# A stack of four graph layers on one core: the third layer's neighbour sum moved ahead of its weights, its bias carried in a column, and every engine's steps in a new sequence

## The chip, the core and the metric

The kernel runs on one core of a Trainium2 chip. A core has five engines that each work through an instruction list of their own: TensorE (PE) for matrix products and transposes, VectorE (DVE), ScalarE (ACT), GpSimd (POOL) and SyncE (SP), which issues most transfers. They meet at semaphores only. The metric is device time in microseconds for the whole launch, the median of several runs.

## What is computed

128 graphs of 128 nodes with 128 features each go through four layers. Each layer adds its result to its input and normalises every node's row to mean 0 and variance 1.

```python
x = _layernorm(x + _L0_gnn_ref(x, adj, ...))   # 25 nodes, 5 groups, two convolutions
x = _layernorm(x + _L1_gnn_ref(x, adj, ...))   # attention, 8 heads, log(adj + 1e-6) added to the scores
x = _layernorm(x + _L2_gnn_ref(x, adj, W, b))  # the layer that is changed here
x = _layernorm(x + _L3_gnn_ref(x, adj, ...))   # 5 rounds of a gated recurrent cell

def _L2_gnn_ref(node_features, adj_matrix, W, b):
    degree = jnp.sum(adj_matrix, axis=-1)
    d_inv_sqrt = jnp.power(degree, -0.5)
    d_inv_sqrt = jnp.where(jnp.isinf(d_inv_sqrt), 0.0, d_inv_sqrt)
    norm_adj = adj_matrix * d_inv_sqrt[:, :, None] * d_inv_sqrt[:, None, :]
    transformed = jnp.einsum('bnf,of->bno', node_features, W) + b
    return jax.nn.relu(jnp.einsum('bnm,bmo->bno', norm_adj, transformed))
```

## The kernel before

Four graphs make a **block**, and two blocks (a = half 0, b = half 1) make an **iteration**; there are 16 iterations and so 32 blocks. A tile of a block is 128 x 512. The loop runs 19 **passes**. In one pass three threads of work run beside each other, on different iterations: thread A is the attention of the iteration before (steps `x1_t`, `qkv`, `s`, `max`, `t`, `p`, `a`, `u`, `n`, `on`, `wo`), thread B is the first layer of the newest iteration and the third layer of the one or two before (`l0_...`, `adj_t`, `x2`, `x2_t`, `l2_t`, `l2_agg`), and thread R is the five rounds of the gated cell (`agg`, `r`, `r2`, `hn`, `in`, `z`, `z2`, `turn`, `begin`, `end`) for two blocks that are two to three rounds apart. The order of each engine's list is written out by hand: `MERGE` holds for each engine two strings of A, B and R, one for each half of a pass, which say from which thread the next step comes. The same two strings serve all 19 passes; in the first and last passes the steps of iterations that don't exist are left out, and a few steps of the last blocks are held back (`HELD`).

The third layer of a block runs so. `x2` (DVE): the second layer's normalised rows. `x2_t`: PE turns them with 4 transposes into the PSUM bank M2 (L958, a helper line for all transposes), ACT copies the result to `x2T` (L620). `l2_t`: PE multiplies by the weights (L1152), DVE adds the bias row out of M2 (`t_b`, L832), POOL multiplies each row by its `dinv` (`t_d`, L526). `l2_agg`: PE sums over the neighbours with `adjT` (L1157), ACT applies the second `dinv` and the relu (L677), DVE adds `x2` (`y3`) and takes the moments for the norm. The bank M2 is shared by all steps of thread B, so they follow each other in it. L996 is the gated cell's products, L1107 the scores, L610 the exponentials, L1124 the weighted sums of the attention, L1140 its output product, L1090 to L1094 the keys, queries and values, L1193 the cell's neighbour sum, L535 and L539 POOL's two operations per round of the cell (`h_lo`, `hd`), L714 a norm on DVE.

Of the kernel before, what the change touches and what calls it, by code (L numbers as in the profile page):

```python
# [7 lines left out]
ALU = mybir.AluOpType  # L8
# [17 lines left out]
LAYERS = 5  # L26
# [13 lines left out]
    deg=NG, deg_safe=2 * NG, deg_pow=NG, dinv=NG, x2t_mm=NG, x2_t=NG, t_mm=NG, t_b=NG, t_d=NG, a_mm=NG, a_relu=NG, y3=NG,  # L40
# [34 lines left out]
def first_third_steps(half):  # L75
    end, last, pair = (1 - half, 1 - half), (2 - half, 1 - half), (0, 0)
    second = [(*last, "x2_t", 0), (*last, "l2_t", 0), (*last, "l2_agg", 0), (*end, "adj_t", 0), (*end, "l0_add", 0)]
# [34 lines left out]
def body_steps(merge):  # L112

    out = []
    for half in range(NG):
        threads = dict(A=iter(attention_steps(half)), B=iter(first_third_steps(half)), R=iter(gated_steps(half)))
        out += [(thread, *next(threads[thread])) for thread in merge[half]]
        assert all(next(left, None) is None for left in threads.values())
    return out
# [9 lines left out]
def gnn_stack_kernel(nc, x, adj, nodemask, W1, b1, W2, b2, fusion_w, Wq, Wk, Wv, Wo, bo, L2W, L2b,  # L129
# [3 lines left out]
    with ExitStack() as ctx:  # L133
# [1153 lines left out]
```

## Time and profile before

| | us |
|---|---|
| three runs | 1687.17, 1689.47, 1689.93 |
| median | 1689.47 |
| span of the profiled execution, first to last instruction | 1687.2 |
| first product for keys in the first block | 34.1 |
| one pass (two blocks) in the steady stage | 99.9 |
| busy: PE, its weight loads, DVE, ACT, POOL | 1619.3, 1343.7, 1400.9, 1314.6, 790.3 |

The first 34 us load and turn the weights; from there to about 200 us the three threads start one after the other; from 200 to about 1500 us each pass has all three and repeats to 0.1 us; after that the threads run out and the last block's cell is alone. The page's busy time counts a PE instruction from its start to its modelled end, so the ends of neighbours overlap; the distance from one start to the next is the time that PE gives to it.

### The profile page before, as it was taken

How to read it: one execution, taken by the hardware profiler on the slowest of the kernel's cores; microseconds unless marked ns; L12 is line 12 of the kernel's file. 1: busy time of each engine (PE TensorE's matmuls, PEld its weight loads, DVE VectorE, ACT ScalarE, POOL GpSimd, SP SyncE). 2: the span in 40 equal slices, each digit the busy share in tenths (PEclk: the TensorE clock that was granted, in tenths of full speed). 3: DMA queues.
4: the chain of work that ended last, by engine and by line, in shares of the span. 5: the costliest groups of instructions: out<-in, count | busy, mean ns of one | idle time of the engine just before them, and what ended most of it. 6: DMA issues, size and time to landing. Idle time of an engine off the chain costs nothing.

```text
span 1687.2 us, 34433 instructions
## 1 busy us (share of the span) xinstructions
PE 1619.3 (96%) x12294; PEld 1343.7 (80%) x12294; DVE 1400.9 (83%) x3563; ACT 1314.6 (78%) x3147; POOL 790.3 (47%) x842
## 2 busy tenths in 40 slices
PE   8789999999999999999999999999999999999997
PEld 7568787887878788787887878888787888877776
DVE  5687888979789897989879798897978889797766
ACT  2568878887878888878887887878787888878766
POOL 3143544536454463544546354453645445354442
PEclk9899999999999999999999999999999999999999
DMA  3010100001010100101001010000101001000000
GB/s 95 20 42 1 30 26 17 27 14 42 14 30 14 28 28 14 30 26 30 14 20 36 14 31 26 18 26 14 43 13 30 25 17 27 14 26 14 13 1 20
DMA packets 84803, 40.97 MB, mean 24 GB/s; under 512 B 10629, under 2 KB 84634, under 8 KB 84634
## 3 DMA queue, kind: packets, MB, share of 16 engines
q1 hardware_dynamic: 84058, 38.62, 8.4%
q8 instruction: 99, 1.62, 0.4%
q14 instruction: 70, 0.57, 0.1%
q10 hardware_dynamic: 576, 0.15, 0.0%
HBM read 30.36 MB, written 8.39 MB: 23 GB/s over the span
## 4 chain that ended last, share of the span: by engine, by line
PE 82%; DVE 8%; ACT 7%; issue 1%; POOL 1%; SPq 0%; DMA 0%; POOLq 0%; DVEq 0%; ACTq 0%
PE RA L996 18%; PE RB L996 17%; PE Q L958 8%; PE RT L1193 8%; PE RT L958 4%; PE Q L1107 4%; PE Q L1124 3%; PE M L958 3%; PE Q L1140 2%; ACT x L553 2%; PE Q L1094 2%; PE Q L1090 2%; PE M L1157 2%; PE M L1152 2%; PE Q L1091 2%; PE M L1035 1%
## 5 line engine op out<-in xcount | busy, mean ns | idle before, releaser
L535 POOL TENSOR_TENSOR h_lo<-hT,h_hi 128x512 fp32r<-128x512 f32 (+1 forms) x163 | 205.9, 1264 | 561.0 <-ACT h_hi L636 488.3
L610 ACT ACTIVATE e_s<-Q,s_ng 128x128 f32<-128x128 f32 x1024 | 292.2, 398 | 42.2 <-DVE s_ng L803 42.1
L539 POOL TENSOR_TENSOR hd<-hT,nn 128x512 f32<-128x512 f32 x156 | 201.0, 1288 | 38.7 <-ACT nn L654 38.7
L811 DVE TENSOR_TENSOR p_s<-Q,adjTe 128x512 f32<-128x512 f32 x256 | 171.2, 684 | 15.5 <-PE Q L958 14.3
L803 DVE TENSOR_REDUCE s_ng<-Q 128x4 f32<-128x512 f32 x256 | 169.1, 682 | 14.0 <-PE Q L1107 12.3
L646 ACT ACTIVATE tr<-RA,b_rz 128x512 f32<-128x512 f32 (+1 forms) x160 | 113.7, 710 | 83.6 <-PE RA L996 83.6
L861 DVE SCALAR_TENSOR_TENSOR un<-tr,un 128x512 f32<-128x512 f32 (+1 forms) x164 | 115.1, 704 | 72.2 <-ACT un L650 71.7
L958 PE MATMUL Q<-ident,e_s 128*128 128x128 f32 x1024 | 154.0, 275 | 10.9 <-ACT e_s L610 10.8
L654 ACT ACTIVATE nn<-tr,wT 128x512 f32<-128x512 f32 (+1 forms) x164 | 118.0, 722 | 57.6 <-DVE tr L866 57.5
L958 PEld LDWEIGHTS Q<-ident,e_s 128*128 128x128 f32 x1024 | 122.3, 141 | 33.1 <-ACT e_s L610 16.6
L488 POOL TENSOR_TENSOR rs<-ve,half_neg 128x4 f32<-128x4 f32 x128 | 140.3, 1096 | 10.7
L996 PE MATMUL RA<-agg_hi,comp_hi 128*128 128x512 f32 (+1 forms) x320 | 140.9, 440 | 2.6 <-DVE agg_lo L856 0.9
L996 PE MATMUL RB<-h_hi,whh_hi 128*128 128x512 f32 (+1 forms) x320 | 143.1, 447 | 0.0
L1193 PE MATMUL RT<-a_bin,h_tok 128*128 128x128 f32 x1008 | 137.1, 279 | 0.6 <-ACT h_tok L634 0.2
L658 ACT ACTIVATE tz<-RB,b_rz 128x512 f32<-128x512 f32 (+1 forms) x160 | 111.8, 699 | 31.0 <-PE RB L996 28.9
L484 POOL TENSOR_SCALAR ve<-mv 128x4 f32<-128x4 f32 x128 | 41.1, 321 | 200.9 <-DVE mv L699 195.5
L1193 PEld LDWEIGHTS RT<-a_bin,h_tok 128*128 128x128 f32 x1008 | 124.7, 191 | 11.8 <-issue 4.6
L856 DVE TENSOR_TENSOR agg_lo<-RT,agg_hi 128x512 fp32r<-128x512 f32 (+1 forms) x159 | 108.3, 681 | 28.4 <-ACT agg_hi L642 24.9
L553 ACT ACTIVATE x<-y,nm,rs 128x128 f32<-128x128 f32 x254 | 104.3, 481 | 32.9 <-DVE nm L710 32.1
L875 DVE SCALAR_TENSOR_TENSOR hd<-tz,hd 128x512 f32<-128x512 f32 (+1 forms) x164 | 120.5, 736 | 7.3 <-ACT tz L658 3.3
L996 PE MATMUL RB<-h_hi,whh_lo 128*128 128x512 f32 (+1 forms) x320 | 125.7, 393 | 0.0
L996 PE MATMUL RA<-agg_lo,comp_hi 128*128 128x512 f32 (+1 forms) x320 | 125.1, 391 | 0.0
(237 smaller groups left out, 4429.2 us busy)
## 6 DMA issues: line engine op xcount, KB each, us to landing
adjn<-in_adj_dram SPq DMA_DIRECT2D x32, 256.0 KB, 2.9
xin<-in_x_dram SPq DMA_DIRECT2D x32, 256.0 KB, 3.4
adjr<-in_adj_dram SPq DMA_DIRECT2D x32, 256.0 KB, 3.1
out_dram<-x SPq DMA_DIRECT2D x32, 256.0 KB, 2.4
adjc<-in_adj_dram SPq DMA_DIRECT2D x124, 4.0 KB, 2.1
xs<-in_x_dram SPq DMA_DIRECT2D x120, 16.0 KB, 1.8
W1s<-in_L_gnn_W_dram SPq DMA_DIRECT2D x1, 640.0 KB, 4.9
W2s<-in_L_gnn_W_dram SPq DMA_DIRECT2D x2, 320.0 KB, 5.0
```

Source lines behind the costliest of these rows:

```text
L488: return pool.tensor_tensor(r[:, :], v[:, :], half_neg[:, 0, 0:GB], ALU.pow)
L535: pool.tensor_tensor(h_lo[g][:, c], hT[g][:, c], h_hi[g][:, c], ALU.subtract).then_inc(SG["h_lo"][g], 1)
L539: pool.tensor_tensor(hd[g][:, c], hT[g][:, c], nn[g][:, c], ALU.subtract).then_inc(SG["hd"][g], 1)
L553: ins = act.activation(o[:, b, :], y[:, b, :], ACT.Identity, bias=n[:, b:b + 1], scale=r[:, b:b + 1])
L610: ins = act.activation(e_s[:, j, c, :], Q[j][:, c * P:(c + 1) * P], ACT.Exp, bias=s_ng[:, j, c:c + 1])
L654: act.activation(nn[g][:, c], tr[g][:, c], ACT.Tanh, bias=bih[:, 2:3]).then_inc(SG["n_act"][g], 1)
L803: dve.tensor_reduce(s_ng[:, j, :], Q[j][:, :].rearrange("p (c k) -> p c k", c=4), AX_X, ALU.max, negate=True)\
L811: dve.tensor_tensor(p_s[:, j, :, :].rearrange("p (b h) q -> p b h q", b=2), Q[j][:, :].rearrange("p (b h q) -> p b h q", b=2, h=2), adjTe[ ...
L875: dve.scalar_tensor_tensor(hd[g][:, c], tz[g][:, c], 1.0, hd[g][:, c], ALU.add, ALU.mult).then_inc(SG["he"][g], 1)
L958: return pe.transpose(o, i, ident[0:rows, 0:rows])
L996: ins = pe.matmul(o[:, cs], weights, moving[:, cs], start=start and i == 0, stop=last is not None and i == len(pairs) - 1)
L1193: ins = pe.matmul(T[:, q * P:(q + 1) * P], src[:, q, :], a_bin[g][:, q, :], start=True, stop=True)
```

## The change

The third layer now sums over the neighbours first. POOL multiplies `x2` by `dinv` into columns 0 to 126 of a new tile `x2d` (step `l2_agg` on POOL, L607), and DVE writes `dinv` itself into column 127 (a second small instruction in step `x2`). PE takes `x2d` as it lies, with the nodes on the partitions, as the stationary side and `adjT` as the moving side (`l2_agg`, L1233), and the sum comes out turned; ACT copies it to `agg2T`; PE multiplies by the weights (`l2_t`, L1238); ACT applies `dinv` and relu as before. The 4 transposes per block, the bias addition on DVE and `t_d` are gone. A normalised row sums to zero, so its last feature is minus the sum of the others: the weights are prepared once with their last input row subtracted from the others (`l2_ext`, one DVE instruction), and the place of the last input row takes the bias, which the `dinv` column then carries through the sum. The pieces below are, in this order, POOL's, ACT's, DVE's (in `x2`, in `l2_t`, and once at the start) and PE's.

```diff
+                elif kind == "l2_agg":
+                    wait(pool, "dinv", it, 2 * g + 2)
+                    wait(pool, "x2", it, g + 1)
+                    pool.tensor_tensor(x2d[:, :, 0:P - 1], x2[g][:, :, 0:P - 1], dinv[g][:, :].unsqueeze(2).broadcast_to([P, GB, P - 1]), ALU.mult)\
+                        .then_inc(S["x2_d"], 1)
                 elif kind == "l2_t":
-                    wait(pool, "t_b", it, g + 1)
-                    wait(pool, "dinv", it, g + 1)
-                    pool.tensor_tensor(t_d[:, :, :], t_b[:, :, :], per_graph(dinv[g][:, :]), ALU.mult).then_inc(S["t_d"], 1)
-                elif kind == "l2_agg":
...
-                elif kind == "x2_t":
-                    wait(act, "x2t_mm", it, g + 1)
-                    act.activation(cols(x2T[g]), M2[:, :], ACT.Copy).then_inc(S["x2_t"], 1)
+                elif kind == "l2_agg":
+                    wait(act, "agg2_mm", it, g + 1)
+                    act.activation(cols(agg2T), M2[:, :], ACT.Copy).then_inc(S["agg2_t"], 1)
...
+                    wait_before(dve, "agg2_mm", it, g)
+                    dve.scalar_tensor_tensor(x2d[:, :, P - 1], deg[g][:, :], 0.0, deg_p[g][:, :], ALU.not_equal, ALU.mult)\
+                        .then_inc(S["dinv"], 1)
...
                 elif kind == "l2_t":
-                    wait(dve, "t_mm", it, g + 1)
-                    dve.tensor_tensor(t_b[:, :, :], M2[:, :].rearrange("p (b d) -> p b d", b=GB),
-                                      l2b_row[:, :].unsqueeze(1).broadcast_to([P, GB, P]), ALU.add).then_inc(S["t_b"], 1)
-                elif kind == "l2_agg":
                     wait(dve, "x2", it, g + 1)
                     wait(dve, "a_relu", it, g + 1)
...
+            dve.wait_ge(w_first, 16 * SQUARE_DMAS)
+            dve.tensor_scalar(l2_ext[:, 0:P - 1], stage[:, WL2, 0:P - 1], stage[:, WL2, P - 1:P], None, ALU.subtract).then_inc(w_ext, 1)
...
-                elif kind == "x2_t":
-                    wait(pe, "x2", it, g + 1)
+                elif kind == "l2_agg":
+                    wait(pe, "dinv", it, 2 * g + 2)
+                    wait(pe, "x2_d", it, g + 1)
...
-                        ins = turn(M2[:, q * P:(q + 1) * P], x2[g][:, q, :])
-                    ins.then_inc(S["x2t_mm"], 1)
+                        ins = pe.matmul(M2[:, q * P:(q + 1) * P], x2d[:, q, :], adjT[g][:, q, :], start=True, stop=True)
+                    ins.then_inc(S["agg2_mm"], 1)
```

At the start the bias transfer moves from the last of SP's weight transfers to the sixth (128 rows of one element in place of a row broadcast to all partitions), and PE turns the third layer's weights, out of `l2_ext`, with its second group of weights and no longer with its first.

The sequence is the second half of the change. `MERGE` has three strings per engine in place of two: one for passes 0 to 4 taken together, one that serves each of passes 5 to 12, one for passes 13 to 18 taken together. Its letters stand for finer lanes (on PE the cell's steps split into gates, `in`, `z` and the rest; on DVE and ACT the two blocks in the cell, and the attention's `max` and `p`, have lanes of their own), so steps can pass each other that had a fixed order.

```diff
+HEAD, TAIL = 5, 13
...
+    head, body, tail = MERGE[engine]
+    blocks = [(range(HEAD), head)] + [(range(n, n + 1), body) for n in range(HEAD, TAIL)] + [(range(TAIL, iters + LAG), tail)]
```

Three places where it shows. First PE in pass 1, between the first and the second block's attention. Before (L1140 is the first block's output product, `Q<-ident,x` the turning of the second block's rows, L1042 and L1046 the first layer's second weights for the next iteration, L1090 to L1107 keys, queries, values and scores of the second block):

```order
L958 MATMUL Q<-ident,o_ns 128x128 x4
L1140 MATMUL Q<-wT,on_ts 128x128 x4
L958 MATMUL Q<-ident,x 128x128 x4
L1042 MATMUL M<-hid_t,W2s 128x200 x2
L1042 MATMUL M<-hid_t,W2s 128x8x9 x2
L1046 MATMUL M<-hid_t,W2s 128x8x7 x2
L1046 MATMUL M<-hid_t,W2s 128x8x6 x4
L1090 MATMUL Q<-xT,wT 128x512
L1091 MATMUL Q<-xT,wT 128x512
L1094 MATMUL Q<-wT,xT 128x128 x4
L1107 MATMUL Q<-km,qT 128x256 x8
```

Now (the lines have moved by 85: L1225 is L1140, L1175 is L1090, L1192 is L1107, L1127 and L1131 are L1042 and L1046, L1120 is the first layer's first weights):

```order
L1225 MATMUL Q<-wT,on_ts 128x128 x4
L1041 MATMUL Q<-ident,x 128x128 x4
L1120 MATMUL M<-y_t,W1s 128x8x9
L1120 MATMUL M<-y_t,W1s 128x8x7
L1120 MATMUL M<-y_t,W1s 128x8x6 x2
L1175 MATMUL Q<-xT,wT 128x512
L1176 MATMUL Q<-xT,wT 128x512
L1179 MATMUL Q<-wT,xT 128x128 x4
L1192 MATMUL Q<-km,qT 128x256 x8
L1127 MATMUL M<-hid_t,W2s 128x200 x2
L1127 MATMUL M<-hid_t,W2s 128x8x9 x2
L1131 MATMUL M<-hid_t,W2s 128x8x7 x2
```

The first layer's second weights have moved from ahead of the second block's keys to behind its scores. Next PE at the end of a steady pass, around the attention's normalisation of block b (`Q<-ident,o_ts` and `Q<-ident,o_ns` are the transposes ahead of and behind it). Before:

```order
L1124 MATMUL Q<-p_s,vp 32x128 x16
L958 MATMUL Q<-ident,o_ts 128x128 x8
L996 MATMUL RB<-h_hi,whh_hi 128x512
L996 MATMUL RB<-h_lo,whh_hi 128x512
L996 MATMUL RB<-h_hi,whh_lo 128x512
L996 MATMUL RB<-agg_hi,comp_hi 128x512
L996 MATMUL RB<-agg_hi,comp_lo 128x512
L996 MATMUL RB<-agg_lo,comp_hi 128x512
L958 MATMUL Q<-ident,o_ns 128x128 x4
L958 MATMUL RT<-ident,x_0 128x128 x4
L1140 MATMUL Q<-wT,on_ts 128x128 x4
```

Now:

```order
L1081 MATMUL RB<-h_hi,whh_hi 128x512
L1081 MATMUL RB<-h_lo,whh_hi 128x512
L1081 MATMUL RB<-h_hi,whh_lo 128x512
L1209 MATMUL Q<-p_s,vp 32x128 x16
L1081 MATMUL RB<-agg_hi,comp_hi 128x512
L1081 MATMUL RB<-agg_hi,comp_lo 128x512
L1081 MATMUL RB<-agg_lo,comp_hi 128x512
L1041 MATMUL Q<-ident,o_ts 128x128 x8
L1041 MATMUL Q<-ident,o_ns 128x128 x4
L1041 MATMUL RT<-ident,x_0 128x128 x4
L1225 MATMUL Q<-wT,on_ts 128x128 x4
```

One of the six gate products' groups now stands ahead of the weighted sums, the other between them and the transposes, and none behind. Last POOL at the start of a steady pass, with the third layer of block b. Before:

```order
L493 TENSOR_SCALAR deg_z<-deg 128x10
L495 TENSOR_TENSOR deg_s<-deg,deg_z 128x10
L497 TENSOR_TENSOR pow<-deg_s,half_neg 128x10
L512 TENSOR_SCALAR adjTe<-adjT 128x512
L516 TENSOR_TENSOR x1b<-x,bo_row 128x512
L535 TENSOR_TENSOR h_lo<-hT,h_hi 128x512
L526 TENSOR_TENSOR t_d<-t_b,dinv 128x512
L539 TENSOR_TENSOR hd<-hT,nn 128x512
```

Now:

```order
L574 TENSOR_SCALAR deg_z<-deg 128x10
L576 TENSOR_TENSOR deg_s<-deg,deg_z 128x10
L578 TENSOR_TENSOR pow<-deg_s,half_neg 128x10
L617 TENSOR_TENSOR h_lo<-hT,h_hi 128x512
L607 TENSOR_TENSOR x2d<-x,dinv 128x4x127
L621 TENSOR_TENSOR hd<-hT,nn 128x512
L593 TENSOR_SCALAR adjTe<-adjT 128x512
```

The multiplication by `dinv` stands at the same place between the cell's two operations, but takes `x2` directly, and `adjTe` and `x1b` have moved behind it.

## Rows read from the trace of the kernel before

**Rows 1.** The page: busy time by engine, and the last chain's shares.
```profile
PE 1619.3 (96%) x12294; PEld 1343.7 (80%) x12294; DVE 1400.9 (83%) x3563; ACT 1314.6 (78%) x3147; POOL 790.3 (47%) x842
...
PE 82%; DVE 8%; ACT 7%; issue 1%; POOL 1%; SPq 0%; DMA 0%; POOLq 0%; DVEq 0%; ACTq 0%
```

**Rows 2.** Busy time by stretch: start, first blocks, one steady pass, the end.
```profile
core 0: us, PE busy (x) PEld busy (x) DVE busy (x) ACT busy (x) POOL busy (x), PEclk, DMA share, GB/s
34.00:69.50 35.50, 25.51 (x224) 19.70 (x224) 24.45 (x67) 16.32 (x52) 7.70 (x12) 0.95 0.09 25
69.50:104.40 34.90, 27.31 (x223) 21.04 (x222) 21.89 (x66) 20.63 (x60) 9.15 (x12) 0.85 0.08 20
...
597.79:697.72 99.93, 98.25 (x753) 81.99 (x753) 86.34 (x219) 81.60 (x196) 49.63 (x52) 1.00 0.09 24
1496.00:1545.70 49.70, 46.96 (x354) 37.97 (x353) 43.23 (x108) 39.52 (x92) 23.97 (x27) 1.00 0.04 12
1545.70:1595.00 49.30, 46.19 (x339) 36.36 (x338) 38.60 (x89) 37.31 (x87) 21.12 (x20) 1.00 0.08 21
1595.00:1687.20 92.20, 78.51 (x489) 64.71 (x487) 56.91 (x146) 60.14 (x127) 30.32 (x31) 0.97 0.04 10
```

**Rows 3.** Timeline of PE in a steady pass: start, length, instruction.
```profile
901.65 0.60 PE L958 MATMUL M<-ident,x 128*128 128x128 f32 x4
902.08 0.60 PE L958 MATMUL RT<-ident,hT 128*128 128x128 f32 x4
...
906.20 0.48 PE L996 MATMUL RB<-h_hi,whh_hi 128*128 128x512 f32 x1
```

**Rows 4.** Groups of the third layer's instructions: busy us, mean ns, idle before.
```profile
L526 POOL TENSOR_TENSOR t_d<-t_b,dinv 128x512 f32<-128x512 f32 x32 | 33.3, 1041 | 35.7 <-DVE t_b L832 35.7
...
L832 DVE TENSOR_TENSOR t_b<-M,l2b_row 128x512 f32<-128x512 f32 x32 | 21.9, 685 | 2.1
L958 PE MATMUL M<-ident,x 128*128 128x128 f32 x128 | 20.0, 280 | 0.1
...
L794 DVE SCALAR_TENSOR_TENSOR dinv<-deg,deg_p 128x4 f32<-128x4 f32 x32 | 4.9, 152 | 0.0
```

**Rows 5.** Timeline at the start, between the first and second block's attention.
```profile
67.21 1.24 PE L1042 MATMUL M<-hid_t,W2s 128*128 128x200 f32 x8
69.61 1.09 PE L1090 MATMUL Q<-xT,wT 128*128 128x512 f32 x2
76.45 0.66 PE L958 MATMUL Q<-ident,e_s 128*128 128x128 f32 x4 [1.39 <-ACT e_s L610]
...
67.41 0.60 ACT L598 ACTIVATE xT<-Q 128x512 f32<-128x512 f32 x1 [0.57 <-PE Q L958]
```

**Rows 6.** Timeline of PE from the end of one steady pass into the next.
```profile
990.12 1.09 PE L958 MATMUL Q<-ident,o_ts 128*128 128x128 f32 x8 [1.05 <-ACT o_ts L614]
...
992.46 0.64 PE L958 MATMUL Q<-ident,o_ns 128*128 128x128 f32 x4
...
1001.59 0.60 PE L958 MATMUL M<-ident,x 128*128 128x128 f32 x4
```

**Rows 7.** Timeline of DVE, POOL and ACT ahead of block b's third layer.
```profile
999.66 1.12 DVE L714 TENSOR_SCALAR x<-y,mv,rs 128x128 f32<-128x128 f32 x4
...
1000.49 1.98 POOL L497 TENSOR_TENSOR pow<-deg_s,half_neg 128x10 f32<-128x10 f32 x1
...
903.32 1.60 POOL L516 TENSOR_TENSOR x1b<-x,bo_row 128x512 f32<-128x512 f32 x1
904.88 1.27 POOL L535 TENSOR_TENSOR h_lo<-hT,h_hi 128x512 fp32r<-128x512 f32 x1
...
903.38 0.64 ACT L636 ACTIVATE h_hi<-hT 128x512 fp32r<-128x512 f32 x1
```

**Rows 8.** Timeline of the start: SP's issue of the third layer's weights, DVE's wait.
```profile
8.26 0.43 SPq L385 DMA_DIRECT2D stage<-in_L_gnn_W_dram  x1
...
16.81 0.69 DVE L784 TENSOR_REDUCE deg<-adjn 128x4 f32<-128x512 f32 x1 [1.96 <-DMA adjn<-in_adj_dram]
```

More of the change, by code:

```diff
@@ L39 @@
     wo_mm=NG, y2=NG,
-    deg=NG, deg_safe=2 * NG, deg_pow=NG, dinv=NG, x2t_mm=NG, x2_t=NG, t_mm=NG, t_b=NG, t_d=NG, a_mm=NG, a_relu=NG, y3=NG,
+    deg=NG, deg_safe=2 * NG, deg_pow=NG, dinv=2 * NG, x2_d=NG, agg2_mm=NG, agg2_t=NG, t_mm=NG, a_relu=NG, y3=NG,
 )
@@ L76, in first_third_steps @@
     end, last, pair = (1 - half, 1 - half), (2 - half, 1 - half), (0, 0)
[L77 removed]
+    second = [(*last, "l2_agg", 0), (*last, "l2_t", 0), (*end, "adj_t", 0), (*end, "l0_add", 0)]
     if half == 0:
@@ L109, in gated_steps @@
     return out
[L112 to L117, printed above, removed]
+THREADS = dict(A=[step for half in range(NG) for step in attention_steps(half)],
+               B=[step for half in range(NG) for step in first_third_steps(half)],
+               R=[step for half in range(NG) for step in gated_steps(half)])
@@ new lines, in lanes, with near_last, held_back @@
+def lanes(engine):
+    out = {}
+    for thread, steps in THREADS.items():
+        for lag, g, kind, k in steps:
+            if kind in KINDS[engine]:
+                out.setdefault(lane(engine, thread, g, kind), []).append((lag, g, kind, k))
+    return out
+LANES = {engine: lanes(engine) for engine in MERGE}
+def near_last(iters):
+    return [(iters - 2, NG - 1), (iters - 1, NG - 2)]
+def held_back(iters):
+    last, (third, second) = (iters - 1, NG - 1), near_last(iters)
+    return dict(
+        vector={(*third, "end", 0): (*last, "x3", 0), (*second, "he", 2): (*last, "agg_lo", 0), (*second, "h_new", 2): (*last, "agg_lo", 0),
+                (*second, "end", 0): (*last, "h_new", LAYERS - 3), (*second, "out", 0): (*last, "agg_lo", LAYERS - 2)},
+        gpsimd={(*second, "end", 0): (*last, "turn", LAYERS - 2)},
+        scalar={(*third, "out", 0): (*last, "z", LAYERS - 3), (*second, "out", 0): (*last, "z", LAYERS - 1)},
+    )
@@ new lines, in sequence @@
+def sequence(engine, iters):
+    held = held_back(iters).get(engine, {})
+    head, body, tail = MERGE[engine]
+    blocks = [(range(HEAD), head)] + [(range(n, n + 1), body) for n in range(HEAD, TAIL)] + [(range(TAIL, iters + LAG), tail)]
+    for passes, merge in blocks:
+        threads = {name: iter([(n, (n - lag, g, kind, k)) for n in passes for lag, g, kind, k in steps if 0 <= n - lag < iters and (n - lag, g, kind, k) not in held])
+                   for name, steps in LANES[engine].items()}
+        for name in merge:
+            yield next(threads[name])
```

149 lines of the change are left out of this document (92 added, 57 removed).

## The prediction

> **What bounds the kernel now.** I read the page first. PE is busy for 1619.3 of 1687.2 us, and 82% of the chain that ended last is PE's own work, with 8% on DVE and 7% on ACT [rows 1]. Then the busy time by stretch [rows 2]. A steady pass takes 99.93 us, of which PE is busy 98.25, DVE 86.34, ACT 81.60 and POOL 49.63. So in the long middle PE is the engine that sets the time, with 1.68 us without work in a pass. The middle alone runs from about 200 to 1500 us. At the ends it is otherwise: from 34 to 104.4 us PE has 9.99 + 7.59 = 17.6 us without work, from 1496 to the end 2.74 + 3.11 + 13.69 = 19.5 us. There the chain from one engine to the next sets the pace, and the order of steps matters more than their sum. Third, the timeline of PE: how far apart do instructions start when nothing is waited for? The 4 transposes of `x2` start at 901.65 and the next step at 902.08: 0.43 us for the four [rows 3]. Each shows 0.60 us from start to end, but the end overlaps with the next step, so 0.43 is the price.
>
> **The change part by part.**
>
> *Transposes.* 4 per block, 32 blocks, gone. By the starts this is 32 x 0.43 = 13.8 us of PE. The group's own busy time is 20.0 us [rows 4], but that holds the overlapping ends; it is the upper end, 13.8 the value. Since PE has 98.25 of 99.93 us busy in a pass [rows 2], nearly all of it is on the path in the middle, two blocks in each pass: 0.86 us per pass. At the two ends it is worth less where PE waits anyway, but there are only 3 passes at either end, so the lower end is what 13 passes of the middle give, 11 us. I take 13.8. The other two products keep their number and shape; only the sides change places.
>
> The Trainium skill, "TensorE: Matmul & The Clock Gate", section "Back-to-back issue gap", gives about 81 ns for a matmul of 128 columns in a stream with its weight load, which makes an estimate of 128 x 81 = 10.4 us. The trace does not agree: 0.43 / 4 = 108 ns [rows 3], and the trace decides.
>
> *DVE.* `t_b` goes: 0.685 us x 32 = 21.9 us [rows 4]. A second `dinv` is added, the same size as the first but for a stride: 0.152 x 32 = 4.9 us. DVE is not the bound in the middle, so the 17 us are no term of the sum; they loosen DVE's list. The new wait for the block before's `agg2_mm` is for a product that lies about half a pass back: nothing.
>
> *POOL.* `t_d` at 1.04 us goes, `x2d` comes. No row shows it; the nearest are `t_d` (1.04 [rows 4]) and `x1b`, also a broadcast in SBUF (1.60 [rows 7]). I take 1.04, the row with the same operand kinds. With POOL at half load this is no term, but its place is a risk (below).
>
> *The chain in M2.* Before: turn, ACT, product, DVE, POOL, sum, ACT. Now: sum, ACT, product, ACT. What stood in the middle (0.685 + 1.04 us and a transposition) goes, and POOL's part moves ahead of the bank. This gives thread B more room; PE hardly waited there before (0.1 us [rows 4]), so it is worth nothing by itself.
>
> *Start.* The bias transfer is issued just behind the third layer's weights, whose issue is at 8.26 and takes 0.43 [rows 8], so the transfers behind it are issued 0.43 us later, while the number of issues ahead of `adjn` stays. DVE must now wait for these weights and do one small instruction. It has 1.96 us without work before `adjn` arrives at 16.81 [rows 8]: that hides it. If the one-element rows land more than about 1.5 us later than the other transfers, that cover is gone, and the start lengthens by the excess, once. I cost it at 0.
>
> *Sequence, first passes.* One place can be worked out. Between the first two blocks of attention, 2.40 us of first-layer products (67.21 to 69.61) stood ahead of the keys, though the keys' input `xT` was copied by 67.41 + 0.60 = 68.01 [rows 5]. They now stand behind the scores, where PE waited 1.39 us for the first exponential [rows 5]. The keys start 1.6 us earlier; what moves behind the scores exceeds the wait and what fills it by some tenths. Gain: between 1 and 2 us of the 9.99 us without work in that stretch, about a sixth.
>
> *Sequence, other ends.* The tables of passes 0 to 4 and 13 to 18 are separate now, so such moves are possible in all of the 17.6 + 19.5 = 37.1 us. I take a sixth there too, 6.2 us with the place above in it. This is a choice by analogy and not a reading; its bounds are 0 and a third, 12.
>
> *Sequence, middle.* At the end of a pass the work between attention sums and output product is reordered. Before, PE waited 1.05 us for `o_ts`, and the six gate products between 991 and 992.4 covered DVE's normalisation up to 992.46 [rows 6]. Now one group of three covers the first wait and none the second. The three that moved ahead are done in any case, so what counts is when `o_ns` starts: by the same durations a few tenths later. Against that, the steps of thread B stand farther from what they wait for. I take 0 for the two together, with +-0.5 us per pass, +-7 in all.
>
> *Sum.* 1687.2 - 13.8 - 6.2 = 1667.2 us of span. The median of the runs, 1689.5, lies 2.3 us above the profiled span, which makes 1669.5; I forecast **1669 us**.
>
> **The rivals.**
>
> *A, forecast: PE's length.* 1669 us, between 1655 and 1683: from 12 us at the ends and 0.5 us per pass better, to 11 us of transposes, nothing at the ends and 0.3 us per pass worse. For it: PE's 98.25 of 99.93 us [rows 2].
>
> *B, the sequence gives more.* PE's waits in the middle are partly hidden in the overlapping ends, so more than 1.68 us per pass may be there to win. If the new sequence takes away one us in each of 14 passes and a third of the ends, the sum is 1689.5 - 13.8 - 14 - 12 = 1650 us. Against it: the order in the middle is nearly the old one, and two of the places where PE waits still stand as tight.
>
> *C, PE is not the limit.* Weight loads are busy only 81.99 of 99.93 us [rows 2]. If PE had room, a ring of ACT, DVE and POOL would set the pass, and PE would only wait longer when its transposes go: 1687 to 1690 us. Against it: in the timeline the steps of PE follow each other at fixed distances, and 82% of the chain is PE's [rows 1]. The Trainium skill, "Perfetto Trace Analysis", section "Identifying the Most-Contended Engine", calls matmul busy time a poor measure of how far a kernel is from its limit, and takes the weight loads' busy share; by that rule PE has 18% of room here, and this rival is what would come.
>
> *D, slower: `x2d` on POOL comes late.* Before, PE needed `x2` only to turn it, at 1001.59 [rows 6], and DVE had it ready at 999.66 + 1.12 = 1000.78 [rows 7]. Now POOL stands in between. In the new order DVE copies `vp` first (as long as `t_b`, 0.69), so `x2` and two `dinv` are there near 1001.8 [rows 4, 7]; POOL is in `pow` until 1002.47, then does `h_lo` (1.27) and `x2d` (1.04 to 1.60): ready at 1004.8 to 1005.4 [rows 4, 7]. PE now has more steps ahead of the sum: the scores, a gate group, the cell's neighbour sum and one gate group more. The first three took from 902.5 to 906.2 in the pass before, with the weights' product of the third layer between them [rows 3], which is taken as long as the gate group that isn't: about 3.7 us, so it asks near 1005.3. This just fits. But `h_lo` itself waits for ACT's `h_hi`, which came 1.5 us after `pow`: at 903.38 + 0.64 = 904.02, that is 1003.95 a pass later [rows 7]. If ACT is not earlier in the new order, `x2d` ends at 1006.3 to 1006.8 and PE waits 1.0 to 1.5 us, in each pass, with `hd` queued behind on POOL and the cell's next round behind that. It turns the whole to slower from about 1.3 us per pass ((13.8 + 6.2) / 16). At the upper end, 1.5 us x 16 = 24 us: 1669 + 24 = 1693 us. Against it: ACT's copies for that turn now stand ahead of the gates' two activations, and only block b has this queue.
>
> **How the numbers follow.** A 0.62, B 0.25, C 0.05, D 0.08. Likeliest is A, so 1669. The range for 8 in 10 takes all of A and B down to 1645: 1645 to 1683. A difference of 0.2%, 3.4 us, is about what a measurement of this kernel can tell from none. Faster by more than that: A, B and a quarter of D, 0.89. Within it: C and some of D, 0.07. Slower: the rest of D, 0.04.
>
> **What would show it.** Right: a steady pass near 99.0 us with PE still busy for some 98% of it, no group `M<-ident,x` any more, and the second block's keys starting near 68 us and not 69.6. B would show as a pass of 98 us or less. C would show as PE's idle time per pass growing by the 0.9 us. D would show as PE waiting for `x2d` on POOL, once per pass and by 1 us or more, and `hd` behind it. I am wrong altogether if the pass gets longer, or if the start before the first keys (34.1 us) moves by more than 1 us.

## The result, and the profile after

The changed kernel is slower by 1.2%: 1708.88 us (1707.82 to 1709.59) against 1688.32 us, a ratio of 1.0122, 95% interval 1.0108 to 1.0137. The forecast was 1669 us. The page answers [rows 1] (busy time by engine; the last chain's shares):

```profile
PE 1618.8 (95%) x12166; PEld 1328.7 (78%) x12166; DVE 1388.7 (81%) x3564; ACT 1317.4 (77%) x3147; POOL 796.5 (47%) x842
...
PE 58%; DVE 24%; ACT 9%; issue 5%; POOL 3%; SPq 0%; DMA 0%; DVEq 0%; POOLq 0%; ACTq 0%
```

PE has 128 transposes less, but hardly any less busy time, and its share of the last chain fell from 82% to 58%, while that of DVE tripled from 8%. Busy time by stretch answers [rows 2], with the stretches cut at the same events (keys of the first, second and third block; two steady passes; keys of the 31st and 32nd block to the end):

```profile
34.00:66.40 32.40, 23.56 (x204) 18.34 (x204) 24.77 (x62) 15.23 (x47) 7.05 (x10) 0.89 0.10 28
66.40:98.40 32.00, 25.74 (x241) 20.08 (x241) 23.84 (x72) 21.83 (x65) 9.22 (x13) 1.00 0.08 21
803.70:905.50 101.80, 97.99 (x745) 80.80 (x746) 85.04 (x219) 82.19 (x196) 50.83 (x52) 1.00 0.08 23
905.50:1008.10 102.60, 99.18 (x745) 82.07 (x743) 84.58 (x219) 81.87 (x196) 50.36 (x52) 0.98 0.09 24
1521.10:1568.40 47.30, 45.45 (x344) 36.66 (x344) 40.59 (x100) 37.39 (x87) 22.84 (x24) 1.00 0.04 12
1568.40:1707.80 139.40, 123.41 (x822) 101.08 (x821) 98.61 (x242) 98.83 (x220) 53.80 (x54) 0.98 0.05 14
```

The ends got shorter: the third block's keys start at 98.4 us and no longer at 104.4, the fifth's at 190.8 against 198.1, and from the last keys to the end it takes 139.4 against 141.5 us. The middle lost all of it and more: from the fifth block's keys to the 31st's, 13 passes, 1330.3 us against 1299.2, that is 102.3 per pass against 99.9. The passes of before repeated to 0.1 us; these take from 100.6 to 104.6 us.

PE also waits for another engine now. From 500 to 1300 us, eight passes, it waited 11.4 us in the kernel before, all of it for two copies of ACT (`o_ts` 8.2, `on_ts` 3.2). In the changed kernel it waits 24.5 us there, and 23.5 of these are for results of DVE (`o_ns` 12.7, the cell's `hT` 6.9 and `agg_lo` 3.7).

The place at the start that the prediction worked out, [rows 5]:

```profile
65.78 0.60 ACT L680 ACTIVATE xT<-Q 128x512 f32<-128x512 f32 x1 [1.69 <-PE Q L1041]
66.43 1.12 PE L1175 MATMUL Q<-xT,wT 128*128 128x512 f32 x2
71.25 1.34 PE L1127 MATMUL M<-hid_t,W2s 128*128 128x200 f32 x8
75.84 0.33 PE L1041 MATMUL Q<-ident,e_s 128*128 128x128 f32 x1 [0.38 <-ACT e_s L692]
```

The keys follow their input at once, and the wait for the exponential is down from 1.39 to 0.38 us. And the third layer's groups, [rows 4] (busy us, mean ns of one, idle before):

```profile
L607 POOL TENSOR_TENSOR x2d<-x,dinv 128x508 f32<-128x508 f32 x32 | 34.6, 1081 | 22.4 <-DVE x2d L879 22.4
L1238 PE MATMUL M<-wT,agg2T 128*128 128x128 f32 x256 | 34.5, 277 | 0.7 <-ACT agg2T L702 0.7
L1233 PE MATMUL M<-adjT,x2d 128*128 128x128 f32 x256 | 34.0, 276 | 0.4 <-POOL x2d L607 0.4
L702 ACT ACTIVATE agg2T<-M 128x512 f32<-128x512 f32 x32 | 19.3, 602 | 1.3 <-PE M L1233 1.3
```

`x2d` costs 1.08 us, close to the estimated 1.04, and PE waits for it 0.4 us in the whole run, and for ACT's copy `agg2T` 0.7 us. Rival D did not happen.

What took its place is in the chain of waits, from the second scores of block b (978.92) to the next keys, some of its pieces:

```profile
978.92 1.12 PE Q L1192 x16
980.06 0.70 DVE s_ng L888
980.79 2.17 ACT e_s L692 x8
...
985.32 0.68 DVE p_s L896
986.00 0.75 DVE hd L956
...
992.84 0.66 DVE agg_lo L937
...
997.50 1.04 DVE y L967 x4
...
1000.04 1.19 DVE nm L792
1001.25 1.66 ACT x L635 x4
1002.95 1.12 PE RT L1041 x4
```

From 985 to 1001 us the chain stays on DVE, one instruction behind the other. In the kernel before PE holds it up to 986 us, and DVE for 4 us only:

```profile
984.49 1.41 PE RA L996 x6
...
985.92 0.69 ACT tr L646
...
987.42 0.70 DVE un L861
...
991.47 1.65 ACT x L553 x4
```

### The profile page after: what moved, and what is told of

Its sections match the earlier page's. It is cut to its first block, busy times and chain, and to the rows that moved or that the text cites. A ratio compares the mean times of both kernels' runs of the same rounds, so it can differ in the third digit from the quotient of the medians.

```text
span 1707.8 us, 34195 instructions
## 1 busy us (share of the span) xinstructions
PE 1618.8 (95%) x12166; PEld 1328.7 (78%) x12166; DVE 1388.7 (81%) x3564; ACT 1317.4 (77%) x3147; POOL 796.5 (47%) x842
## 4 chain that ended last, share of the span: by engine, by line
PE 58%; DVE 24%; ACT 9%; issue 5%; POOL 3%; SPq 0%; DMA 0%; DVEq 0%; POOLq 0%; ACTq 0%
PE RA L1081 12%; PE RB L1081 11%; PE Q L1041 6%; PE RT L1274 5%; PE RT L1041 4%; PE Q L1192 4%; ACT e_s L692 3%; DVE stats L778 2%; DVE s_ng L888 2%; DVE hd L956 2%; DVE un L942 2%; DVE p_s L896 2%; PE Q L1209 2%; DVE tr L947 2%; DVE hT L960 2%
## 5 line engine op out<-in xcount | busy, mean ns | idle before, releaser
L1081 PE MATMUL RA<-agg_hi,comp_hi 128*128 128x512 f32 (+1 forms) x320 | 145.4, 454 | 12.2 <-DVE agg_lo L937 10.2
L956 DVE SCALAR_TENSOR_TENSOR hd<-tz,hd 128x512 f32<-128x512 f32 (+1 forms) x164 | 116.0, 709 | 46.4 <-POOL hd L621 32.3
L1041 PE MATMUL Q<-ident,e_s 128*128 128x128 f32 x1024 | 147.9, 275 | 5.3 <-ACT e_s L692 5.3
L942 DVE SCALAR_TENSOR_TENSOR un<-tr,un 128x512 f32<-128x512 f32 (+1 forms) x164 | 120.3, 735 | 31.7 <-ACT un L732 30.2
L569 POOL TENSOR_TENSOR rs<-ve,half_neg 128x4 f32<-128x4 f32 x128 | 135.9, 1062 | 10.7
L1081 PE MATMUL RB<-h_lo,whh_hi 128*128 128x512 f32 (+1 forms) x320 | 125.2, 391 | 0.0
L1081 PE MATMUL RA<-agg_hi,comp_lo 128*128 128x512 f32 (+1 forms) x320 | 124.7, 390 | 0.0
```

The source lines that it names most:

```text
L569: return pool.tensor_tensor(r[:, :], v[:, :], half_neg[:, 0, 0:GB], ALU.pow)
L942: dve.scalar_tensor_tensor(un[g][:, c], tr[g][:, c], 1.0, un[g][:, c], ALU.add, ALU.mult).then_inc(SG["rv"][g], 1)
L956: dve.scalar_tensor_tensor(hd[g][:, c], tz[g][:, c], 1.0, hd[g][:, c], ALU.add, ALU.mult).then_inc(SG["he"][g], 1)
L1041: return pe.transpose(o, i, ident[0:rows, 0:rows])
L1081: ins = pe.matmul(o[:, cs], weights, moving[:, cs], start=start and i == 0, stop=last is not None and i == len(pairs) - 1)
```

## The experiments

All times stand against runs of the kernel before on the same chip, 1687.9 to 1689.2 us. Where runs of two groups are set beside each other below, up to 1.3 us of the difference may come from that.

### Old order, new arithmetic

First the arithmetic alone: the two old strings per engine set all passes, and each old place of the third layer takes the new step that belongs there. PE's sum takes the old product's place and the product the old sum's; ACT's copy takes the place that was nobody's on ACT, between two exponentials; POOL's `x2d` takes the place of the turn.

```diff
+OLD_KIND = dict(
+    tensor={"x2_t": None, "l2_t": "l2_agg", "l2_agg": "l2_t"},
+    scalar={"x2_t": None, "l2_t": "l2_agg", "l2_agg": "l2_t"},
+    vector={"x2_t": None, "l2_t": None, "l2_agg": "l2_t"},
+    gpsimd={"x2_t": "l2_agg", "l2_t": None, "l2_agg": "l2_t"},
+)
```

> The changed third layer in the sequence of before, in all passes and on all four engines: PE's sum stands where the weights' product stood, the product where the sum stood, POOL's multiplication where the x2 transposes had their letter. Theory S (the new sequence of the steady passes loses, the arithmetic wins): a steady pass of 99.93 - 0.86 = about 99.1 us, the start of before (second block's keys at 69.6 us), in all 1688 - 12 = 1676 us, between 1671 and 1682. Rival M (the multiplication on POOL between x2 and PE costs more than the transposes did): a pass of 100.5 us or more and 1695 us or more.

1764.42 us, ratio 1.0456 (1.0440 to 1.0471). PE waits for `x2d` in block b, 24.4 us in 8 passes, at most 3.1 us. So D's mechanism is real where POOL has `adjTe`, `x1b` and `h_lo` ahead of it. With passes 0 to 4 in the new order:

```diff
-OLD_IN = {e: ("head", "body", "tail") for e in MERGE}
+OLD_IN = {e: ("body", "tail") for e in MERGE}
```

> The changed third layer with the new sequence in passes 0 to 4 alone, and the sequence of before in all later passes. Theory S: the start keeps what the changed kernel's trace shows (fifth block's keys at 190.8 and not 198.1 us), the steady pass is about 99.1 us: 1688 - 12 - 7 = 1669 us, between 1664 and 1675, which would beat both kernels. Rival (the gain of the start is given back when the old sequence takes over, since the engines' lists stand differently there): 1676 us as without the new head. Rival M: 1690 us or more.

1749.13 us, 1.0365 (1.0349 to 1.0380). The new start is worth 15.3 us here; the old middle still waits for `x2d`.

### The changed kernel, one place at a time

First the end of a pass, where PE waits for `o_ns` now ([rows 6] had a wait of 1.05 us for `o_ts` and none here):

```profile
797.92 0.34 PE L1041 MATMUL Q<-ident,o_ns 128*128 128x128 f32 x1 [1.88 <-DVE o_ns L907]
```

PE gets its old interleaving back there; then, by itself, DVE's `nm` goes behind the attention's `u` and `n`:

```diff
-             "BRRRTBAIABTZZRRRITZAZAAATA"),
+             "BRRRTBAIABTZZRRRITAAAZZATA"),
```

> The changed kernel with one edit: in the body's PE string the two gate groups z and z2 stand again behind the transposes of o_ts and ahead of those of o_ns, as before. Theory P (at the pass end PE has nothing left to cover DVE's normalisation): PE's idle time ahead of o_ns goes, 1 to 2 us in each of the 8 body passes, and with it the drops of the granted clock at these places: 1690 to 1700 us. Rival D (DVE's list is what is late in the whole pass, so that PE would wait elsewhere): 1704 to 1709 us, with PE waiting for hT and agg_lo instead.

1711.75 us, 1.0138 (1.0123 to 1.0153), above both ranges. At the end of a pass PE now waits 1.02 us for `o_ts`, 0.95 for `o_ns`, 0.71 for `x`, 0.45 for `h_lo`.

```diff
-             "RRRAAARASCRAS"),
+             "RRAAAARRSCRAS"),
```

> The changed kernel with one edit: in the body's DVE string the small instruction of step x3 (nm, 128x4) stands behind the four instructions of the attention's normalisation and no longer ahead of them. In the changed kernel it took 1.2 us while POOL was in hd, and den waited behind it. Theory P2 (this one small instruction makes den late): about 1 us in each of the 8 body passes, 1695 to 1702 us. Rival (den is late for other reasons, or x3 and begin are then late in its place): 1705 to 1711 us.

1707.47 us, 1.0119 (1.0102 to 1.0136). PE's wait for `o_ns` is down to 0.96 us, and PE waits 1.10 us for `x` instead.

Without POOL's multiplication, in the new order and then in the old:

```diff
-                    pool.tensor_tensor(x2d[:, :, 0:P - 1], x2[g][:, :, 0:P - 1], dinv[g][:, :].unsqueeze(2)...
-                        .then_inc(S["x2_d"], 1)
...
-                    wait(pe, "x2_d", it, g + 1)
+                    wait(pe, "x2", it, g + 1)
```

> The changed kernel with POOL's multiplication x2d left out (the product sums x2 itself, so the degrees' scaling on the left is missing). Theory D (x2d is late or crowds POOL and so costs the middle): the 31 us that the middle lost come back, about 1675 us. Theory S (the new order of the middle passes loses by itself, at the waits of the cell's hT on DVE and of o_ns at the pass's end): within 5 us of the changed kernel, 1703 to 1710 us, with PE still waiting about 1.2 us for hT in each pass 22 us behind block a's keys.

1708.6 us, 1.0110 (1.0095 to 1.0125): POOL's step costs the changed kernel nothing.

> The new arithmetic in the old order of steps (as the first experiment, 1764 us), with POOL's multiplication left out. There PE waited 25.7 us in 8 passes ahead of the sum for x2d. If x2d's lateness is all that the old order lost with the new arithmetic: the old pass less PE's four transposes per block, 99.1 us, about 1676 us in all. If the sum ahead of the product itself lengthens the chain in M2 (PE waits for agg2T): above 1690 us.

1698.18 us, 1.0051 (1.0036 to 1.0066), pass 100.59: the second of the two. With neither `x2d` nor the transposes the old order is still 0.66 us per pass slower than before, and PE waits 8.4 us in 8 passes for `agg2T`, ACT's copy. Next POOL's `x2d` of block b was made early:

```diff
+    step = (2, 1, "l2_agg", 0)
+    rest = [s for s in steps if s != step]
+    at = rest.index((0, 0, "l0_deg", 0)) + 1
+    return rest[:at] + [step] + rest[at:]
```

> The whole new arithmetic in the old order, with one step moved: POOL does block b's x2d right behind l0_deg, ahead of te, x1b and h_lo. Prediction's step (transposes are worth 13.8 us where PE is the bound) with theory S: 1673 to 1680 us, faster than the kernel before, pass near 99.1 us. Theory D in its strong form (x2d cannot be ready in time in any order, since x2 itself comes too late): above 1695 us, PE still waiting 1 us or more for x2d per pass.

1704.46 us, 1.0088 (1.0071 to 1.0105), pass 100.97. Neither theory: PE waits for `x2d` no more, but for `agg2T` 11.2 us in 8 passes. With the new start (passes 0 to 4):

> As the one with x2d moved to the front, but passes 0 to 4 in the new order. The new start was 5.9 us earlier at the third block's keys and 7.3 us at the fifth's. If that gain is the start's own: 6 to 8 us below the kernel of the old order in all passes, about 1668 us. If the gain at the start is only lent (work pushed behind into the middle): equal to it within 2 us.

1699.7 us, 1.0058 (1.0043 to 1.0073): 4.8 us less, between the two theories. Then PE's product was put one exponential's turn and one gate group later:

```diff
+    for step, behind in (((2, 1, "l2_t", 0), (3, 1, "r", 3)), ((1, 0, "l2_t", 0), (2, 0, "r", 4))):
+        out.remove(step)
+        out.insert(out.index(behind) + 1, step)
```

> As the kernel with x2d moved to the front and passes 0 to 4 in the new order (1699.7 us, pass 100.97 us); moved besides: PE does the product with the weights behind the turn of the next exponential and one gate group, so ACT has time to copy agg2T. There PE waited about 0.7 us for that copy in each block, 1.4 us per pass. If the transposes are worth their length wherever PE finds no new wait: the pass falls by 1.4 us to 99.6 us or less, 13 passes of the old order and the tail, about 1682 us, faster than before. If the wait only moves (to the relu's bank or the adjacency's turn behind it): 1695 to 1700 us.

1701.78 us, 1.0079 (1.0063 to 1.0095), pass 101.11. The wait did move, and the pass got no shorter. Groups of ACT's relu and PE's product from 500 to 1300 us, first ahead of the move (old order in all passes), then behind it:

```profile
L818 ACT ACTIVATE a_r<-M,dinv 128x128 f32<-128x128 f32 x64 | 19.2, 429 | 5.4 <-PE M L1297 5.4
L1297 PE MATMUL M<-wT,agg2T 128*128 128x128 f32 x128 | 18.5, 288 | 11.2 <-ACT agg2T L761 11.2
```

```profile
L827 ACT ACTIVATE a_r<-M,dinv 128x128 f32<-128x128 f32 x64 | 18.2, 368 | 12.1 <-PE M L1306 12.1
...
L1306 PE MATMUL M<-wT,agg2T 128*128 128x128 f32 x128 | 16.8, 274 | 0.0
```

Either PE waits for ACT's copy, or ACT for PE's product. In the second case what stands behind the relu in ACT's list is late, and PE waits for that in its turn: 3.6 us for the cell's `tr` and 3.2 us for exponentials in 8 passes, where it had no such waits ahead of the move.

Three more at single waits of the new order: POOL's `end0` ahead of its last `hd`, DVE's `a_c` behind the cell's `hd` and `hT`, and both. The first pair of lines is POOL's string, the second DVE's.

```diff
-            ("BSCRARSADSDCRRSSSRAARSSCRRSASRDCDSRRA"),
+            ("BSCRARSADSDCRRSSSRAARSSCRRSASRDCDRSRA"),
...
-            ("RBACMMRBBRMMBSRRPBCSPPSPCRBSSBCMRBRMSMMPCRRSPPSPRSSSASSAAASRSRARRSAMMMMSSRPSSCPRRPPSRRSMMBSMMRPPSSCCRRCSPPRRSS"
+            ("RBACMMRBBRMMBSRRPBCSPPSPCRSSBBCMRBRMSMMPCRRSPPSPRSSSASSAAASRSRARRSAMMMMSSRPSSCPRRPPSRRSMMBSMMRPPSSCCRRCSPPRRSS"
```

> The changed kernel, with one swap on POOL in the middle passes: end0 (ve, rs) ahead of block b's last hd, as in the old order. Theory K (DVE's small nm, 1.26 us at the pass's end and 0.15 before, stands still while POOL's hd runs, and o_ns, one us late for it, ends the pass late): nm falls to 0.15 us there, o_ns comes 1 us earlier, and the eight middle passes are 1 to 2 us shorter each, with fewer stretches at half clock: 1693 to 1701 us. Theory R (a ring of waits through DVE sets the pass, and a wait taken away at one place comes back at another, as with the two edits of the pass's end before): 1706 to 1710 us.

1709.39 us, 1.0125 (1.0109 to 1.0141). `nm` is short, PE's wait for `o_ns` is 1 us less, and the next keys wait for `xT` in their turn:

```profile
1003.11 0.15 DVE L792 SCALAR_TENSOR_TENSOR nm<-mv,rs 128x4 f32<-128x4 f32 x1
...
1010.70 1.12 PE L1175 MATMUL Q<-xT,wT 128*128 128x512 f32 x2 [1.17 <-ACT xT L680]
```

> The changed kernel, with one move on DVE in the middle passes: the first layer's a_c (1.84 us at 925.8) behind the cell's hd and hT instead of ahead of them. PE waits 1.17 us for that hT in each pass, 22 us behind block a's keys. If the wait is on the path: 1.2 us in each of 8 passes, about 1699 us. Theory R: 1706 to 1710 us, the wait gone at that place and found at another.

1708.81 us, 1.0123 (1.0105 to 1.0142); the wait for `hT` is half gone, 0.52 us where it was 0.92.

> Both moves together. If each wait is on the path by itself: the sum of both gains, 1685 to 1692 us. Theory R: 1705 us or more. If the two waits are one slack shared between them: no more than the larger gain of the two.

1707.67 us, 1.0114 (1.0098 to 1.0130). These are four moves, alone or two together, at PE's waits for `o_ns` and `hT`. The five kernels take 1707.5 to 1711.8 us against 1708.9, and none gains 2 us: a wait of PE is not the price of the place where it shows.

### Who copies the sum

First a run that asks whether PE was the limit at all:

> The kernel before, with three of the four transposes of x2 left out in each block (so three quarters of x2T hold old values); order, waits and all other instructions stay. The prediction's price, 0.108 us for each transpose on the path: 32 x 3 x 0.108 = 10.4 us less, 1677 us to 1679 us, pass 99.28 us. Theory C (PE is not the limit): 1686 to 1690 us, pass 99.9 us.

```diff
-                    for q in range(GB):
+                    for q in range(1):
                         ins = turn(M2[:, q * P:(q + 1) * P], x2[g][:, q, :])
```

1677.97 us, 0.9938 (0.9923 to 0.9952), pass 99.28 us. Six transposes fewer shorten a pass by 0.65 us, 0.108 each, while PE's waits stay as they were (11.3 us in 8 passes, 11.4 before): PE was the limit before. Over the whole launch it is 11.2 us for 96 transposes, 0.117 each.

Then the new arithmetic in the old order, with `x2d` early, and the copy of the sum given to DVE:

> The new arithmetic in the old order with x2d moved to the front of POOL's list (1704.5 us, pass 100.97), and the copy of the neighbours' sum out of M2 is DVE's, at the place where its bias addition stood, no longer ACT's. Theory T (ACT's copy has moved from ahead of the scores to between the exponentials, where ACT sets the pace, and this eats the transposes' gain): the pass falls to 99.0 to 99.4 us and the whole to 1673 to 1682 us, faster than before. Theory C (PE is no limit and the transposes are worth nothing): 1686 to 1690 us. If the later sum is late for every engine: 1695 us or more.

```diff
+                elif kind == "l2_copy":
+                    wait(dve, "agg2_mm", it, g + 1)
+                    dve.tensor_copy(cols(agg2T), M2[:, :]).then_inc(S["agg2_t"], 1)
...
-    scalar={"x2_t": None, "l2_t": "l2_agg", "l2_agg": "l2_t"},
-    vector={"x2_t": None, "l2_t": None, "l2_agg": "l2_t"},
+    scalar={"x2_t": None, "l2_t": None, "l2_agg": "l2_t"},
+    vector={"x2_t": None, "l2_t": "l2_copy", "l2_agg": "l2_t"},
```

1675.31 us, 0.9919 (0.9903 to 0.9936). Against the same with ACT's copy (1704.46 us), one copy on another engine makes 29.2 us of difference, and the arithmetic with DVE's copy is worth 13.9 us. The pass is 99.04 us, and PE waits at neither product (a window from one block a's keys to the next; groups from 500 to 1300 us):

```profile
792.99:892.03 99.04, 97.35 (x745) 81.15 (x744) 87.28 (x220) 80.52 (x195) 50.17 (x51) 1.00 0.09 24
...
L818 ACT ACTIVATE a_r<-M,dinv 128x128 f32<-128x128 f32 x68 | 20.3, 427 | 1.8 <-PE M L1300 1.8
L1300 PE MATMUL M<-wT,agg2T 128*128 128x128 f32 x136 | 18.0, 275 | 0.0
...
L976 DVE COPY agg2T<-M 128x512 f32<-128x512 f32 x17 | 11.5, 676 | 0.0
```

Why ACT's copy costs so much is seen in ACT's timeline. Before, the copy of the turned `x2` came ahead of the first exponential, which had to wait for the scores anyway (0.53 us); from there ACT has work for 5 us without a gap:

```profile
970.02 0.63 ACT L620 ACTIVATE x2T<-M 128x512 f32<-128x512 f32 x1
...
972.18 2.17 ACT L610 ACTIVATE e_s<-Q,s_ng 128x128 f32<-128x128 f32 x8 [0.53 <-DVE s_ng L803]
...
977.27 1.14 ACT L677 ACTIVATE a_r<-M,dinv 128x128 f32<-128x128 f32 x4 [0.22 <-PE M L1157]
```

With the sum first there is nothing to copy before the scores; the copy falls among the exponentials and has PE's product and the relu behind it (old order, `x2d` early):

```profile
882.34 1.20 ACT L751 ACTIVATE e_s<-Q,s_ng 128x128 f32<-128x128 f32 x4
883.34 0.69 ACT L761 ACTIVATE agg2T<-M 128x512 f32<-128x512 f32 x1
...
885.28 1.14 ACT L818 ACTIVATE a_r<-M,dinv 128x128 f32<-128x128 f32 x4 [0.67 <-PE M L1297]
886.29 1.16 ACT L751 ACTIVATE e_s<-Q,s_ng 128x128 f32<-128x128 f32 x4
```

What this costs shows at PE, which has one and the same list in the two runs. Sum, product and the step behind it in block a, with ACT's copy:

```profile
879.16 1.05 PE L1292 MATMUL M<-adjT,x2d 128*128 128x128 f32 x8
...
884.08 1.16 PE L1297 MATMUL M<-wT,agg2T 128*128 128x128 f32 x8 [0.69 <-ACT agg2T L761]
885.08 0.60 PE L1100 MATMUL Q<-ident,e_s 128*128 128x128 f32 x4
```

Sum and the step behind the product, with DVE's:

```profile
864.90 1.05 PE L1295 MATMUL M<-adjT,x2d 128*128 128x128 f32 x8
...
869.86 0.60 PE L1103 MATMUL Q<-ident,e_s 128*128 128x128 f32 x4
```

From the sum to that step it takes 5.92 us and 4.96 us; in block b 5.48 and 4.50. These two differences, 0.96 and 0.98 us, are, but for rounding, the whole 1.93 us by which the pass is longer with ACT's copy (100.97 less 99.04).

A copy of that size at that place in the kernel before, for nobody:

```diff
+                elif kind == "l2_t":
+                    wait(act, "x2_t", it, g + 1)
+                    act.activation(cols(spare), cols(x2T[g]), ACT.Copy)
```

> The kernel before with one more copy on ACT in each block: x2T from SBUF to an unused tile, 0.6 us, between the second and the third exponential, where the changed arithmetic in the old order has its copy of the sum; nobody waits for it. If ACT's time between the exponentials sets the pace there: 0.6 to 1.2 us more per pass at least, 1698 to 1720 us. If the copy costs only because PE waits for its result: within 3 us of the kernel before.

1695.81 us, 1.0041 (1.0027 to 1.0054), pass 100.39: between the two. A copy more in ACT's list costs 0.46 us per pass, and elsewhere: PE waits 2.0 us in 8 passes for the cell's `hT`, for which it did not wait before. The copy of the sum is no copy more than before, and it costs 1.93 us because PE waits for it. No run moved it within ACT's list, so whether an earlier place there would do as well as DVE's is not shown.

The copy on DVE in the new order:

```diff
+            if engine == "scalar" and step[2] == "l2_agg" and step[:2] != (0, 0):
+                continue
...
+            if engine == "vector" and (g, kind, k) == (0, "in", 0):
+                yield n, (it, 1, "l2_copy", 0)
+            if engine == "vector" and (g, kind, k) == (0, "agg_lo", 4) and it + 1 < iters:
+                yield n, (it + 1, 0, "l2_copy", 0)
```

> The changed kernel in its own order, with the copy of the neighbours' sum given from ACT to DVE. Theory T for the new order: the 31 us of the middle come back in large part, below 1695 us. If DVE's own list is what sets the new pass (the chain of the middle stands on DVE for 20 us at the end of each pass): no better than the changed kernel, 1705 to 1720 us.

1728.91 us, 1.0237 (1.0222 to 1.0253), above both ranges: 20.0 us more than the changed kernel, 1.25 in each of 16 passes. Two copies of 0.68 us make 1.36, so the new order pays nearly their whole length, and PE's waits for DVE grow from 23.5 to 34.2 us in 8 passes. DVE's list has no room for the copy there. What ACT's copy costs in the new order is not told by this run, nor by another. Two tenths of a pass of the changed kernel (the busy times are PE, its weight loads, DVE, ACT, POOL):

```profile
824.06:834.24 10.18, 9.26 (x80) 7.28 (x70) 10.11 (x27) 7.31 (x19) 8.58 (x11) 1.00 0.17 52
...
895.32:905.50 10.18, 7.88 (x78) 6.00 (x77) 9.14 (x35) 7.75 (x16) 6.76 (x9) 1.00 0.03 8
```

In the first of them DVE has 0.07 us left of 10.18, in the second PE 2.3. Last the new start (passes 0 to 4), on top of the old order with the copy on DVE:

> As the kernel before in this group, with passes 0 to 4 in the new order (ACT copies there). Theory T with the start's gain its own: 5 us below the kernel before in this group, 1668 to 1677 us. If the start's gain is lent: no difference.

1675.02 us, 0.9921 (0.9906 to 0.9936): no gain. Its fifth keys start 6.4 us earlier than in the old order (190.6 for 197.0), and its two next passes, still in the new order, take 102.5 us each. So the new order was kept only up to pass 2 and from pass 16 on:

```diff
+FIRST_OLD, LAST_OLD = 3, 15
...
+            if not FIRST_OLD <= n <= LAST_OLD:
+                yield n, step
```

> The new arithmetic in the old order, x2d first on POOL, the copy of the sum on DVE (1675.3 us), but passes 0 to 2 and those from 16 on in the changed kernel's order (ACT copies there). With passes 0 to 4 in the new order the fifth block's keys were 6.4 us earlier (190.6 against 197.0 us) and all of it was lost in the next two passes of the new order (102.5 against 99.0 us). If the order of the middle is what loses: keys of the fifth block near 190.6 us, then passes of 99.0 us, and the end 1 to 2 us earlier: 1666 to 1670 us. If the start's gain is lent whatever order follows: 1674 to 1676 us.

1669.68 us (1668.69 to 1670.69), ratio 0.9883 (0.9870 to 0.9897), faster than both kernels. The start keeps some 4 of its 6 us (fifth keys at 192.7 us), the end gives 1.9. That the time is the forecast's is no proof of the forecast: this is another kernel.

## Why the prediction was wrong

- *What bounds the kernel before: right.* PE does; taking transposes away and nothing else shortens every pass (99.28 us). The Trainium skill's rule on the weight loads' busy share ("Perfetto Trace Analysis", "Identifying the Most-Contended Engine"), which gave PE 18% of room, is not borne out by that run.
- *Transposes, 13.8 us: right.* The arithmetic in the old order, with the copy on DVE, brought 13.9, and a pass of 99.0 us as forecast; the price of one transpose in a steady pass was 0.108 us, as read.
- *The chain in M2, "worth nothing by itself": this step failed.* It counted what went out of the chain and named ACT's copy in the new one, but gave it no price. ACT has 18 us without work in a pass, but not where the copy now stands: in the old order the copy costs 29.2 us, more than twice the gain. Before, it stood ahead of the scores, where ACT had to wait anyway; the question that the prediction put to the start (what hides it, and what if that cover is gone) wasn't put to it. How much of this price is in the changed kernel is not shown: in the new order PE waits for the copy 0.7 us in all.
- *Sequence, ends, 6.2 us: right in size, but given back.* With the old middle behind them, three new passes at either end are worth 5.6 us. The 6.2 was a choice by analogy, so part of that is luck. In the changed kernel the gain is outweighed by the slower passes between. At the place that was worked out the keys follow their input at once, which is the 1.6 us of the forecast; the second keys come 3.2 us earlier because the input `xT` itself is copied by 66.38 and no longer by 68.01 us, which the prediction did not see.
- *Sequence, middle, 0 +- 7 us: this step failed too, and it is the one that the changed kernel's own trace shows.* Forecast was a pass near 99.0 us, give or take 0.5; it takes 102.3. With the copy on ACT in both, the old order's pass takes 100.97 us and the new one's 102.3: the new order is no remedy for the copy, and the changed kernel is 9.2 us above the one with the old middle and end. The term looked at one place, `o_ns`, and there too only at PE's rows: for "a few tenths later" PE waits 1.9 us. What a new order does to DVE's list was left out because DVE "is not the bound in the middle": on average over a pass, yes, but nearly all of PE's waits in the new middle are for DVE.
- *POOL and the start, 0: right.* Without `x2d` the changed kernel takes the same time, and the first keys stand at 34.1 us. D's price of 1.0 to 1.5 us was worked out for the new order and is not tested by the 3.1 us of the old one, where POOL has `adjTe` and `x1b` (0.62 and 1.60 us) ahead of it besides.
- *Rivals.* B was refuted, D not what happened. C was wrong on the kernel before, but comes near to what the changed one has become: PE waits longer, and the chain leaves PE for DVE and ACT at the end of each pass. That was held to be no more than a loss of the gain.

The sum, in measured steps: 1689.2 before, -13.9 for the arithmetic with DVE's copy, +29.2 for the copy on ACT, -4.8 for the new start, +9.2 for the new middle and end: 1708.9. They were taken in this order, and are not the same in another: in the new order DVE's copy costs 20 us. So the 29.2 is not shown to be the copy's share of the changed kernel's loss. Shown is that the old order with DVE's copy in passes 3 to 15 takes back 39.2 us of it (1708.9 to 1669.7). Open is which steps of the new middle would have to move: four were tried, alone or two together, and none helped.

## What to carry to other kernels

When a rewrite moves a copy from one place of a chain to another, price it at the place where it will stand in its engine's list, and ask who waits for it there; an engine's mean load does not tell. An engine that is idle for a sixth of a pass, as DVE here, can hold the chain for 16 us of it, and then waits removed one by one come back at another place. Test arithmetic and order apart: here each half had a good part, and the good parts together, with the copy on DVE, made the fastest kernel.

## What the runs showed of the hardware

A small instruction of DVE can last as long as an operation of POOL on a whole tile beside it. `nm`, 128 x 4, takes 0.15 us alone and 1.26 beside POOL's `hd`; the next instructions of DVE are late by the difference (start, length):

```profile
999.95 1.26 DVE L792 SCALAR_TENSOR_TENSOR nm<-mv,rs 128x4 f32<-128x4 f32 x1
```

```profile
999.62 1.58 POOL L621 TENSOR_TENSOR hd<-hT,nn 128x512 f32<-128x512 f32 x1
```

In the same way `a_row`, 128 x 320, went from 0.49 us in the old order to 1.36 in eight passes of the new. It is nothing new of this order: in the kernel before, the `nm` at 992.53 takes 1.23 us beside `hd` (992.47, 1.27 us), but there PE waits for nothing of DVE. The Trainium skill, "SBUF — State Buffer", section "SBUF: two separate sides", tells of a port pair that DVE, with two inputs in SBUF, and GpSimd lock against each other for a whole instruction; the trace agrees: `nm` ends 0.01 us after `hd`.

PE's granted clock fell from 2.4 to 1.2 GHz for a time at five places in the middle of the changed kernel: at four of them PE had just waited 1.9 us for `o_ns` (near 695, 798, 1002 and 1105 us), at one 1.7 us for `hT` (1391 us). Behind an equal wait for `o_ns` near 901 us it did not fall. The kernel before has a granted clock of 1.00 in every steady slice. The two slices around 797.92 (granted clock third from the end, a mean of both levels):

```profile
790.00:795.00 5.00, 4.91 (x51) 3.19 (x49) 4.83 (x13) 2.69 (x4) 4.50 (x8) 1.00 0.10 21
795.00:800.00 5.00, 3.12 (x19) 2.52 (x19) 4.57 (x17) 3.14 (x7) 3.09 (x4) 0.81 0.05 13
```

The kernel with both moves (POOL's swap and DVE's `a_c`) has no such slice and takes about the same time, 1707.67 us: the clock is not the cause either.
